# Wide attention with its features regrouped as 128 + 64, and queries and keys projected in pairs of blocks

## What is computed

```python
def attention(x, w_qkv, w_out):
    qkv = x @ w_qkv
    q, k, v = jnp.split(qkv, [NQ * HD, (NQ + NKV) * HD], axis=-1)
    ...
    q = apply_rope(q, cos, sin)
    k = apply_rope(k, cos, sin)
    k = jnp.repeat(k, REP, axis=2)
    v = jnp.repeat(v, REP, axis=2)
    ...
    attn = jax.nn.softmax(scores, axis=-1)
    out = jnp.einsum('bhqk,bhkd->bhqd', attn, v)
    ...
    return out @ w_out
h = x + attention(rms_norm(x, norm1_w), w_qkv, w_out)
```

## Time and profile before

| | us |
|---|---|
| three runs | 827.0, 830.12, 830.42 |
| median | 830.12 |
| profiled execution, its own time | 827.48 |
| span of its trace | 825.6 |
| mean granted TensorE clock | 0.985 of full speed |

### The profile page before, as it was taken

One profiled execution on the slowest core, in us unless ns is written; L12 is line 12 of the kernel. 1 busy time (PEld: TensorE's weight loads), 2 busy tenths in 40 slices (PEclk: granted clock), 3 DMA queues, 4 the chain that ended last, 5 costly groups with the idle time before them and its releaser, 6 DMA issues. The chain is left out here.

```text
span 825.6 us, 17410 instructions
## 1 busy us (share of the span) xinstructions
PE 766.2 (93%) x6307; PEld 527.9 (64%) x6308; DVE 449.5 (54%) x943; ACT 364.1 (44%) x778; POOL 176.2 (21%) x191
## 2 busy tenths in 40 slices
PE   6999889899999999999899789999999999998997
PEld 4666657677775545555477467765688677674564
DVE  5657667877854634444377667760103477633231
ACT  2266642543532044444264864434060545432553
POOL 0462105535600134443100020000000200001152
PEclk9999999999999899999999999999999999988999
DMA  9021100000003299111340004771000054403110
GB/s 319 14 41 24 22 2 11 16 18 22 11 12 118 78 309 309 49 44 42 101 111 0 1 1 89 181 162 32 1 1 1 13 118 90 118 2 109 36 51 32
DMA packets 84740, 56.02 MB, mean 68 GB/s; under 512 B 56918, under 2 KB 77692, under 8 KB 84672
## 3 DMA queue, kind: packets, MB, share of 16 engines
q1 hardware_dynamic: 77136, 42.98, 20.2%
q0 software_dynamic: 3520, 7.87, 3.3%
q10 hardware_dynamic: 4016, 4.23, 1.5%
HBM read 45.77 MB, written 9.30 MB: 67 GB/s over the span
## 5 line engine op out<-in xcount | busy, mean ns | idle before, releaser
L80 PE MATMUL banks<-con 128*128 128x512 f32 (+1 forms) x228 | 101.8, 561 | 2.9 <-DVEq L2325 1.4
L80 PEld LDWEIGHTS banks<-con 128*128 128x128 f32 x228 | 42.6, 202 | 31.0 <-issue 27.7
L155 ACT ACTIVATE ln_sq<-x 96x544 f32<-96x544 f32 x32 | 20.9, 654 | 86.1 <-DVE x L147 86.0
L690 PE MATMUL banks<-x,a_wqkv 96*96 96x272 f32 x192 | 48.0, 395 | 0.0
L1218 DVE TENSOR_TENSOR a_kx<-a_k,con 96x1632 f32<-96x1632 f32 x21 | 38.7, 1850 | 7.9 <-ACT a_k L995 7.7
L1183 POOL MEMSET a_q<- 96x60 f32 x3 | 0.4, 147 | 180.9 <-POOLq L2640 90.7
L165 PE MATMUL banks<-ln_sq,con 96*96 96x272 f32 x128 | 35.6, 400 | 3.5 <-ACT ln_sq L155 3.4
L2197 POOL DMA_INDIRECT moe_xs<-moe_x_rows,moe_taken x25 | 24.8, 992 | 65.5 <-PE banks L1990 43.5
L2009 PE MATMUL banks<-moe_wu,moe_xf 128*64 x100 | 37.4, 497 | 1.0 <-ACT moe_xf L2134 1.0
L141 PE MATMUL banks<-h,con 96*96 96x272 f32 x128 | 35.3, 398 | 3.2 <-DVE h L2579 1.0
L690 PEld LDWEIGHTS banks<-x,a_wqkv 96*96 96x96 f32 x192 | 30.4, 163 | 11.6 <-issue 0.3
(11 more groups left out here) (435 smaller groups left out, 1907.5 us busy)
## 6 DMA issues: line engine op xcount, KB each, us to landing
moe_wu<-in_moe_up SPq DMA_DIRECT2D x16, 576.0 KB, 5.0
f_w<-in_f_e SPq DMA_DIRECT2D x10, 576.0 KB, 8.3
moe_wd<-in_moe_down SPq DMA_DIRECT2D x16, 288.0 KB, 6.5
patch_px<-in_patches SPq DMA_DIRECT2D x4, 768.0 KB, 10.6
a_vt<-a_v_rows SPq DMA_DIRECT2D x72, 36.0 KB
a_v_rows<-a_vtok SPq DMA_DIRECT2D x24, 96.0 KB, 1.9
f_wu<-in_f_up SPq DMA_DIRECT2D x4, 576.0 KB
f_wd<-in_f_down SPq DMA_DIRECT2D x4, 576.0 KB
```

Of the source, the lines that this page charges most:

```text
L80: self.nc.tensor.matmul(self.ps[bank][:, 0:width], self.ident, self.con[:, 0:width], start=True, stop=True)
L690: last = nc.tensor.matmul(ps[2 + m][0:HD, 0:CW], wqkv[:, a, j * D + m * HD:j * D + (m + 1) * HD], chunk(x, c)[:, a], start=a == 0, stop=a ...
```

## The change

- Weights: `wq` and `wk` become one tile `wqk` of 128 partitions. Its first nine blocks hold the rows of features 0 to 127. Five more blocks hold features 128 to 191: block 0 alone on partitions 0 to 63, then the pairs (1,2), (3,4), (5,6), (7,8), the first of a pair on partitions 0 to 63, the second on 64 to 127. The values' weights stay in halves of 96.
- Activations: per chunk three DMAs inside SBUF. One puts features 96 to 127 on the unused partitions 96 to 127 of `x2`'s first half; two put features 128 to 191 into `x_low`, once on partitions 0 to 63 and once on 64 to 127 (two chunks' room). Chunk 0's are issued by SP at the end of the narrow attention, chunk 1's at the start of the wide stage, chunk c + 2's behind `read_values(c)`.
- Products: a pair makes two 128-row products, one into each bank, then two 64-row products, one into each bank. It waits until both banks are free: for `taken` of block t - 1, and in chunk 0 for `cos_done` of block t - 1 as well.
- Order: chunk 0 goes 0, (1,2), (3,4), (5,6), (7,8), 9, with 512 columns of filler behind each but the first. In the later chunks block 1 leaves its place ahead of the mean; pairs follow steps 0, 2 and 4 of the first group and step 0 of the second, the values step 1. ACT evicts both blocks of a pair in a row.

The diff, where context is left out:

```diff
--- before.py
+++ after.py
@@ -224,13 +224,23 @@
 
 class WideWeights(Weights):
     def allocate(self):
-        self.wq, self.wk = self.sb("wq", [HD, 2, QH * WD]), self.sb("wk", [HD, 2, KVH * 2 * WD])
+        NB = QH // 2 + KVH
+        self.wqk = self.sb("wqk", [128, 128 * (NB + (NB + 1) // 2)])
+        self.x_high, self.x_low = self.env.whole[1][:, 0], self.sb("x_low", [128, 2, CW])
+        self.regrouped = [self.sem("regrouped0"), self.sem("regrouped1")]
         self.wv, self.wo = self.sb("wv", [HD, 2, KVH * WD]), self.sb("wo", [128, QH // 2, D])
         self.w_in = self.sem("w_in")
 
     def load(self, sp):
-        for n, w in (("wq", self.wq), ("wk", self.wk), ("wv", self.wv), ("wo", self.wo)):
+        for n, w in (("wqk", self.wqk), ("wv", self.wv), ("wo", self.wo)):
             sp.dma_start(w[:], self.dram[n]).then_inc(self.w_in, 16)
+
+    def regroup(self, sp, norm, c):
+        x2, cut = self.env.x2, slice(c * CW, (c + 1) * CW)
+        sp.wait_ge(norm.ready, 2 * (c + 1))
+        sp.dma_start(self.x_high[HD:, cut], x2[0:128 - HD, 1, cut]).then_inc(self.regrouped[c % 2], 16)
+        for u in range(2):
+            sp.dma_start(self.x_low[64 * u:64 * (u + 1), c % 2], x2[128 - HD:, 1, cut]).then_inc(self.regrouped[c % 2], 16)
 
 
...
@@ -568,7 +578,7 @@
-def stage_narrow_attention(env, name, weights, rms=False, quantum=False, response=None, ahead=(), before=None, left=0, first_rms=None, router=None):
+def stage_narrow_attention(env, name, weights, rms=False, quantum=False, response=None, ahead=(), before=None, left=0, first_rms=None, router=None, regroup=None):
     nc = env.nc
     x, ps = env.x, env.ps
     HP = HN + 1 if quantum else HN
@@ -677,6 +687,8 @@
                     read_values(c + 1)
                 for w in ahead:
                     w.load_part(sp, c)
+            if regroup is not None:
+                regroup(sp, ln, 0, 2)
 
...
@@ -1421,7 +1433,7 @@
         def sem(n):
             return env.sem(name + "_" + n)
 
-        wq, wk, wv, wo, w_in = weights.wq, weights.wk, weights.wv, weights.wo, weights.w_in
+        wqk, wv, wo, w_in, regrouped = weights.wqk, weights.wv, weights.wo, weights.w_in, weights.regrouped
...
@@ -1472,33 +1484,50 @@
                     sp.dma_start(vt[SLOT * g:SLOT * g + N + 1, c % 2],
                                  bass.AP(v_rows.tensor, c * (CW + 1) * D + g * WD, [[D, N + 1], [N * D, IC], [1, WD]])).then_inc(v_in[c % 2], 16)
 
+            weights.regroup(sp, n1, 1)
             sp.wait_ge(zeroed, 1)
             sp.dma_start(v_rows[:, CW:CW + 1].rearrange("c t d -> t c d"), vt[0:1, 0, 0:NC * KVH].rearrange("p (c g) d -> p c (g d)", c=NC)).then_inc(v_padded, 16)
             sp.wait_ge(v_padded, 16)
             for c in range(NC):
                 write_values(c)
                 read_values(c)
+                if c + 2 < NC:
+                    sp.wait_ge(projected, NT * (c + 1))
+                    weights.regroup(sp, n1, c + 2)
             for w in ahead:
                 w.load(sp)
 
         @block.tensor
         def _(pe):
             def project(c, t):
+                pair = t % 2 and t < TQK
                 if t == 0:
+                    pe.wait_ge(regrouped[c % 2], 48 * (c // 2 + 1))
                     pe.wait_ge(n1.ready, 2 * (c + 1))
-                if t >= 2:
-                    pe.wait_ge(taken, NT * c + t - 1)
-                    if c == 0 and t - 2 < TQK:
-                        pe.wait_ge(cos_done, t - 1)
+                if pair and c >= 1:
+                    pe.wait_ge(taken, NT * c + t)
+                    if c >= 2 and t == 1:
+                        pe.wait_ge(added, 2 * (c - 2) + 2)
+                elif t >= 2 or pair:
+                    done = t if pair else t - 1
+                    pe.wait_ge(taken, NT * c + done)
+                    if t - 2 < TQK:
+                        pe.wait_ge(cos_done, done)
                 elif c == 1:
                     pe.wait_ge(taken, NT)
                 elif c >= 2:
                     pe.wait_ge(added, 2 * (c - 2) + t + 1)
                 to = ps[2 + t % 2]
                 if t < TQK:
-                    w, at = (wq, 128 * t) if t < JQ else (wk, 128 * (t - JQ))
-                    for a in range(2):
-                        last = nc.tensor.matmul(to[:, 0:CW], w[:, a, at:at + 128], chunk(x2, c)[:, a], start=a == 0, stop=a == 1)
+                    some = (t, t + 1) if pair else (t,)
+                    high, low = weights.x_high[:, c * CW:(c + 1) * CW], weights.x_low[:, c % 2]
+                    for n in some:
+                        nc.tensor.matmul(ps[2 + n % 2][:, 0:CW], wqk[:, 128 * n:128 * (n + 1)], high, start=True, stop=False)
+                    for u, n in enumerate(some):
+                        rows, at = slice(64 * u, 64 * (u + 1)), 128 * (TQK + (t + 1) // 2)
+                        last = nc.tensor.matmul(ps[2 + n % 2][:, 0:CW], wqk[rows, at:at + 128], low[rows], start=False, stop=True)
+                        if n < t + len(some) - 1:
+                            last.then_inc(projected, 1)
                 else:
                     for u in range(2):
                         for a in range(2):
@@ -1560,15 +1589,15 @@
                                                 start=j == 0, stop=j == JQ - 1)
                     last.then_inc(out_ready, 1)
 
-            pe.wait_ge(w_in, 64)
-            for t in range(NT):
+            pe.wait_ge(w_in, 48)
+            for t in (0, 1, 3, 5, 7, TQK):
                 project(0, t)
                 if t == 1:
                     before.mean(pe, L)
-                if t == 4:
+                if t == 3:
                     before.var(pe, L)
                 if t >= 1:
-                    env.idle_products(1, 6, 256)
+                    env.idle_products(1, 6)
             scores(0)
             for c in range(NC):
                 more = c + 1 < NC
@@ -1581,8 +1610,6 @@
                     n2.mean(pe, c - 1)
                 if not more:
                     env.idle_products(3, 0)
-                if more:
-                    project(c + 1, 1)
                 if c + 2 < NC:
                     n1.mean(pe, c + 2)
                 if not more:
@@ -1590,9 +1617,9 @@
                     pe.wait_ge(n2.ready, 2 * (c - 1))
                 for u in range(6):
                     weigh(2 * c, u)
-                    if more:
-                        project(c + 1, 2 + u)
-                    elif u < ROUTED:
+                    if more and u % 2 == 0:
+                        project(c + 1, 1 + u)
+                    if not more and u < ROUTED:
                         env.route_early(pe, router, x2, 0, u, u + 1)
                 if not more:
                     pe.wait_ge(n2.ready, 2 * c)
@@ -1600,8 +1627,8 @@
                     if not more and ROUTED + u < EARLY:
                         env.route_early(pe, router, x2, 0, ROUTED + u, ROUTED + u + 1)
                     weigh(2 * c + 1, u)
-                    if more and 8 + u < NT:
-                        project(c + 1, 8 + u)
+                    if more and u < 2:
+                        project(c + 1, (7, TQK)[u])
                 project_out(c, (0,))
                 if more:
                     scores(2 * c + 2)
@@ -1661,20 +1688,22 @@
                     n1.square(act, c + 2)
                 if c >= 1:
                     n2.factor(act, c - 1)
-                if more:
-                    take(c + 1, 1)
                 if c + 2 < NC:
                     n1.factor(act, c + 2)
                 for u in range(6):
                     move_weighed(2 * c, u)
-                    if more:
+                    if more and u % 2 == 0:
+                        take(c + 1, 1 + u)
                         take(c + 1, 2 + u)
                     if u == 2:
                         exponent(2 * c + 1)
                 for u in range(6):
                     move_weighed(2 * c + 1, u)
-                    if more and 8 + u < NT:
-                        take(c + 1, 8 + u)
+                    if more and u == 0:
+                        take(c + 1, 7)
+                        take(c + 1, 8)
+                    if more and u == 1:
+                        take(c + 1, TQK)
...
@@ -3112,7 +3141,8 @@
             env.end_stage()
             n1 = Rms(env, "g0_n1", env.x, env.x2, cols(env, "n1w"), 0, early=True)
             n1.sq, n1.rs = env.sq2, env.rs2
-            last = stage_narrow_attention(env, "a0", a0, rms=True, response=response, before=last, left=1, first_rms=n1)
+            last = stage_narrow_attention(env, "a0", a0, rms=True, response=response, before=last, left=1, first_rms=n1,
+                                          regroup=lambda sp, norm, first, n: g0.regroup(sp, n1, 0))
...
@@ -3154,9 +3184,13 @@
     a["a0_wqkv"] = halves(g["L0_attn_qkv_w"].T)
     a["a0_wo"] = halves(g["L0_attn_proj_w"].T)
     w = g["L0_ffn_w_qkv"]
-    a["g0_wq"] = halves(w[:, 0:QH * WD])
-    wk = w[:, QH * WD:(QH + KVH) * WD].reshape(D, KVH, 1, WD)
```

(8 more changed lines are left out.)

## The result

The changed kernel takes 842.5 us (median of 6 runs, 839.73 to 844.44) against 830.31 us of the kernel before (6 runs, 827.0 to 835.75): a ratio of 1.0149, 95% interval 1.0117 to 1.0181. It is 12.2 us slower. The profiled execution took 839.73 us, with a span of 837.8.

What follows compares the result with a forecast made beforehand. The prediction took chunk 0 of the wide attention, where DVE's chain would run in turn with TensorE, as decisive: 0.7 + 5.7 + 1.8 = +8.2 us, 835.7 profiled, forecast 838 us, range 830.5 to 845.

Steps and rivals of the forecast that it cites:

- The regrouping DMAs, chunk 0: End of narrow attention: the first product waits for the third transfer, +0.7 us, bounds 0 and 2 us.
- a turn of 4.85: Chunk 0, one pair's start to the next: DVE's chain runs in turn with PE, 4.85 us for two blocks.
- The term of 5.7: Chunk 0, first product to first scores: 23.55 us instead of 17.85, +5.7 us, bounds +4.5 to +7.2.
- A = 1.85 us: Chunk 0: ACT's eviction starts 1.85 us behind the pair's start, made of 1.37, 0.09 and 0.39.
- a turn of 5.3: Chunk 0: upper bound from one pair's start to the next if 64-row products are not side by side, 0.46 more.
- A pair 1.66 us, change of form 0.29: TensorE, each pair: six slots of 1.37 us plus 0.29 for switching form, saving 0.17 us, not 0.46.
- Chunks 1 to 3: Later chunks: pairs wait only for evictions; +0.6 us a chunk, 1.8 in all, bounds -0.7 to +1.2 each.
- the exponent of the second group stands behind blocks 3 and 4: ACT, chunks 1 to 3: exponent 1.4 us later, of which 0.9 comes back from block 1, leaving +0.5.
- the clock falls in chunk 0: Rival, chunk 0: PE at 1.2 GHz, a pair costs 1.4 us more, +3 us, 841 us; chance 0.17.
- Not side by side: Rival: 64-row products don't overlap, +0.46 us a pair, 842 us; chance 0.05.
- Waits mostly hidden: Rival: low-end chunk 0, no start delay, later chunks give back 0.7 each, +2.4 us, 832.5 us; chance 0.13.
- Faster because PE sets the pace: Rival: PE's streaming bounds everywhere; 16 pairs save 7.3 us without switch cost (823), 2.7 with it; chance 0.05.

Runs made afterwards that it cites:

- e7: Kernel before plus the three regrouping DMAs per chunk and TensorE's wait for them, old products kept: 832.62 us, ratio 1.0028.
- e3: Changed kernel with more filler in chunk 0, 512 columns after block 0 and two times 512 after each pair: 838.39 us, ratio 1.0103.
- e4: Changed kernel with both 64-row products of a pair on rows 0 to 63, so not side by side: 843.68 us, ratio 1.0185.
- e8: Kernel before with only the changed kernel's waits and fillers in chunk 0, old products, no DMAs: 834.41 us, ratio 1.0056.
- e9: Changed kernel with high and low product of block t first, then those of t+1, inside each pair: 861.71 us, ratio 1.0405.
- e6: Kernel before with block 1 of each following chunk moved from the gap to behind the first transposes: 833.02 us, ratio 1.0027.
- e1: Changed kernel with chunk 0 block by block, old order, waits and fillers, split products kept: 841.15 us, ratio 1.0148.
- e2: Changed kernel with chunk 0's DVE cosine product reading the evicted copy, so pairs wait only for evictions: 839.18 us, ratio 1.0107.
- e10: Changed kernel with e3's filler and four more filler products in the first cycle's gap, where block 1 stood: 837.62 us, ratio 1.0114.
- e11: Changed kernel with e9's order, e2's cosine product and e10's filler together: 844.38 us, ratio 1.0182.
- e5: Kernel before, unchanged, run and traced once more as a control: 829.94 us, ratio 1.0024.
- e12: Kernel before with two 512-column filler products in the first cycle's gap, after block 1: 827.87 us against 828.43, ratio 0.9974.

## Why the prediction was right or wrong

The direction was right and 842.5 lies in the range (830.5 to 845.0), 4.5 us above the forecast of 838.0. Most of those 4.5 us are the clock, which the forecast had in a rival and in the upper bound, not in its sum.

**The regrouping DMAs, chunk 0: forecast +0.7, measured +1.28 (e7 alone: +1.25).** The step was right in kind and its size was off. SP's issues take 0.63 us and 1.23 for two, 0.62 each, where I took 0.38 from the issues of other transfers; two of them stand ahead of the third, which makes 0.5 us. From the third issue (123.71) to the first product it is 2.2 us, where I took 2.1. That regrouping the other chunks is free held.

**Chunk 0: forecast 23.55 us and a turn of 4.85.** At full clock the turns are 4.76, 4.83 and (e3) 4.82; block 0 takes 2.89 to the first pair (forecast 2.8). With the last turn as forecast, 6.2, chunk 0 would take 23.5 us: +5.65. No trace has the changed kernel's last turn at full clock; e4's is 6.33, more than forecast because the last filler takes 1.05 us up to the scores and not 0.86. By that it is +5.8. The term of 5.7 held, as did the releaser. But my explanation was incomplete: I put it all down to DVE's chain "in turn with" PE. e8 has that same wait and loses 3.07 us. The remaining 2.6 are some 0.65 a turn, because block t is complete late when both 128-row products go first (e9's turns of 4.32 and 4.37 bear that out); my own figure A = 1.85 us contained it, but I didn't name it as a cost of the *grouping*. And my upper bound, a turn of 5.3 if the 64-row products were not side by side, was wrong: e4's turn is 4.83. This matters: on PE alone the overlap saves 0.46 us a pair (e4), but in chunk 0 it saves nothing, and the grouping that it needs costs 0.5 (against e9) to 0.65 us (against e8) a turn.

**A pair 1.66 us, change of form 0.29.** Measured 1.69, and 0.32 over its six slots. The rule in the Trainium skill, page "TensorEngine Tiling (Array Packing)", section "Key Properties", that changing the mode drains the array agrees with this and with e9's 0.71 for two round trips. The 64-row products were to start within 10 ns of each other; in the pair at 194.01 they start 6 and 7 ns apart, and e4 shows what the overlap is worth. The 2x that the Trainium skill gives in the section "Theoretical Speedup" of the same page holds for the two low slots alone (0.46 us saved) and is mostly eaten by the change.

**Chunks 1 to 3: forecast +0.6 each, measured +0.16 and +0.10** for chunks 2 and 3; the first cycle can't be read for its clock, see below. This step failed: "the exponent of the second group stands behind blocks 3 and 4: +0.5". Timelines of ACT and DVE in the changed kernel, to be held against the earlier trace rows:

```profile
197.38 0.69 ACT L1649 ACTIVATE g_raw<-banks 128x272 f32<-128x272 f32 x2 [1.14 <-PE banks L1528]
197.96 0.89 ACT L1658 ACTIVATE g_s<-g_s 102x816 f32<-102x816 f32 x1
198.87 1.00 DVE L1774 TENSOR_REDUCE g_sm<-g_s 102x16 f32<-102x816 f32 x1 [0.43 <-ACT g_s L1658]
```

The exponent comes 9.36 us after that of the first group (188.60), where it was 9.30. It does stand behind two evictions, but the second pair starts at 195.51, 2.88 us after the transposes' start at 192.63, not 3.1; from the first of its evictions to the exponent it is 0.58 us, not 0.85; and block 1, absent from the gap, gave back what was left. I had added these with rounding on the high side each time. e6 shows that moving block 1 is free in the steady chunks.

**The rival "the clock falls in chunk 0" came true beside the forecast,** not in place of it. Its price was well sized: the first turn took 6.55 instead of 4.82, the last 7.62 instead of 6.2 (6.33 by e4), together +3.0 to +3.15 us where I had put +3. With 5.65 and 3.15, or 5.8 and 3.0, the +8.80 of the table is whole, the last turn's split being worked out and not measured. Its chance of 0.17 was too low: of the nine traces whose first product waits for the transfers (changed, e1, e2, e3, e4, e7, e9, e10, e11), all but e3 have a slow stretch that begins between 125 and 129 us, and before, e5, e6, e8 and e12, where it doesn't, have none in chunk 0. What goes ahead of it is in the chunk-0 rows above: PE waits 1.94 us for the transfers and 1.55 us behind block 0. I had argued from the fillers in the turns and overlooked these two waits. The runs point to the first: e8 has the second wait alone (1.55 us) and no slow stretch in chunk 0, while e1 and e7 have the first (2.10 and 1.92 us) without the second, and slow stretches of 6.8 and 3.4 us. Of the three kernels with filler behind block 0, e3 stayed at full clock, e10 had 3.4 us at 1.2 GHz and e11 13.7; so the fillers' part in chunk 0 is not settled.

**The first cycle's +2.46** is a slow stretch too (158.9, 6.8 us) and I did not foresee it. With filler in the gap that block 1 left it is gone, in e10 and in e11. The kernel before falls into the same hole in some executions (e5), so only part of it belongs to the change.

**How much of the 12.2 us is clock?** Every execution comes with its mean granted clock. One line fitted through 164 executions of the kernels here, with a constant for each kernel, gives 0.63 us for each 0.001 of clock, with a scatter of about 1.2 us. At a clock of 0.985 it puts the kernel before at 827.8 us, the changed one at 836.0 (e7 830.0, e8 830.5, e6 828.9, e1 831.9, e2 834.6, e3 835.6, e4 837.4, e10 836.7, e11 843.6, e12 827.1). So some 8.2 us are the change's waits and transfers, and some 4.4 go with the lower clock (0.9747 against 0.9818 on average). The table's terms give 1.28 + 5.65 + 0.26 = 7.2 for the first kind, and where the other 1 us lies is open. My sum of 8.2 was for the first kind alone; that the fit gives the same is partly luck, since my start was 0.6 us too small and my later chunks 1.5 too large. At equal clock e1 is 4 us better than the changed kernel, which its median hid. This is a fit and not an experiment; that each kernel's own clock is a result of its gaps is shown only for the first cycle, by e10 and e11 against the seven traces with the gap left empty.

**The other rivals.** *Not side by side*: excluded by e4. *Waits mostly hidden*: the start and chunk 0 took their whole price, and the later chunks gave nothing back (+0.16 and +0.10, where it had -0.7 each). *Faster because PE sets the pace*: e4 and e9 show that in chunks 2 and 3 a part of TensorE's time does reach the end, 0.6 of 1.84 us and 2.0 of 3.4; but 4 pairs of 1.69 leave no saving to pass on once block 1 has moved in (6.76 against 6.42 us).

## What to carry to other kernels

To pack a pair's short products side by side, its long products go first, and then the first block is ready for its eviction 1.84 us after the pair's start, against 1.33 block by block (e9) and 1.19 with the old products (e8). So where two banks take turns between TensorE and the engines that empty them, sum the chain from the moment *the first block is complete*, and compare it with the block-by-block order, before counting saved slots. Put products of the same form next to each other: to and fro in one pair costs 0.3 us of TensorE, and alternating within it 0.7. A wait inserted where TensorE used to be fed can have a second price in the clock behind it, and a trace taken once may show the kernel before without a slow stretch that it often has; compare time and mean clock over several executions before assigning a difference to a cause.

## What was not expected of the hardware

In e2 DVE's cosine product reads SBUF instead of PSUM. It takes the same 443 ns, but POOL's sine product beside it takes 975 ns instead of 717, and DVE's sum, which meets it, 959 instead of 702. Groups by line in chunk 0, changed kernel and then e2:

```profile
L1756 DVE TENSOR_TENSOR g_q<-g_raw,g_swapped 128x272 f32<-128x272 f32 x6 | 4.2, 702 | 0.0
...
L1726 POOL TENSOR_TENSOR g_swapped<-g_swapped,con 128x272 f32<-128x272 f32 x8 | 5.7, 717 | 16.5 <-DVE g_swapped L1742 16.5
```

```profile
L1754 DVE TENSOR_TENSOR g_q<-g_raw,g_swapped 128x272 f32<-128x272 f32 x6 | 5.8, 959 | 0.0
...
L1724 POOL TENSOR_TENSOR g_swapped<-g_swapped,con 128x272 f32<-128x272 f32 x8 | 7.8, 975 | 11.6 <-DVE g_swapped L1740 11.6
```

So moving an operand from PSUM to SBUF on DVE slows POOL and then DVE itself: the price of e2's freed banks. The Trainium skill, page "GPSIMD Engine Reference", section "1. Specifications", says that the two engines share their SBUF interface, with contention when DVE has two inputs from SBUF; these rows agree.

The other surprise is e9: 37.5 us at 1.2 GHz with PE recorded busy for 36.88 of them. A busy engine at the low level did not get the high one back for longer than in any other trace here, where the stretches are 3.4 to 13.7 us. What tells e9 from the rest in this was not found.
